# Graph queries and values as high and low products, values masked once a pair through DRAM, and edge steps spread

## The reference, cut to what matters

```python
self_feat = concat(v, q) @ W_self.T + b_self            # q is 0 where a row of v sums to 0
for d in range(2):                                      # d = 1 uses the transposed adjacency
    A = adj if d == 0 else swapaxes(adj, 1, 2)
    A = A[:, :, :20, :]
    cond, vb = A.sum(-1), A @ w_bias + b_bias           # 11 labels a cell: the "edges"
    kv = self_feat[:, :20]
    qh = (self_feat @ Wq[d].T + bq[d]).reshape(B, N, 16, 8)
    kh = (kv @ Wk[d].T + bk[d]).reshape(B, 20, 16, 8)
    aff = einsum('bnhd,bmhd->bnhm', qh, kh) / sqrt(8)
    aff = where(cond > 0, aff, NEG) + vb
    w = softmax(aff, axis=-1)
    out_t = einsum('bnhm,bmf->bnhf', w, kv)
    output += einsum('bnhf,hgf->bnhg', out_t, Wout[d]) + bout[d]
result = v + relu(output)
```

## Time and profile before

| | |
|---|---|
| median of 3 runs | 608.84 us (607.85 to 609.20) |
| the profiled execution, its own time | 608.95 us |
| its span | 607.4 us |
| granted TensorE clock, mean | 0.998 |
| instructions in the span | 17246 |
| HBM read, written | 25.74 MB, 6.31 MB |

### The profile page before, as it was taken

The page is one execution under the profiler, slowest core; times in us unless marked ns, Lnnn a source line. Parts: engine busy times, 40 slices in busy tenths (PEclk is TensorE's granted clock), DMA queues, the critical chain, the costliest instruction groups (busy, mean ns, idle before and its releaser), DMA issues.

```text
span 607.4 us, 17246 instructions
## 1 busy us (share of the span) xinstructions
PE 594.2 (98%) x5570; PEld 538.0 (89%) x5570; DVE 514.0 (85%) x1132; ACT 466.5 (77%) x1703; POOL 291.1 (48%) x355
## 2 busy tenths in 40 slices
PE   8999999999999999999999999999998999999996
PEld 8889999999999999999999999888887888888886
DVE  5899989888988988998998998888867878888876
ACT  4888887988889789789889879778776566566563
POOL 4445435435435435345354354556643554554551
PEclk9999999999999999999999999999999999999999
DMA  8210210210210210210201202133421212212101
GB/s 239 82 40 9 49 50 10 57 46 9 56 41 15 56 37 19 56 31 24 56 13 42 64 2 57 53 96 105 131 86 54 69 38 71 60 44 69 54 17 36
DMA packets 54678, 32.55 MB, mean 54 GB/s; under 512 B 15200, under 2 KB 52464, under 8 KB 54640
## 3 DMA queue, kind: packets, MB, share of 16 engines
q1 hardware_dynamic: 53008, 27.85, 16.9%
q0 software_dynamic: 1632, 4.21, 2.2%
HBM read 25.74 MB, written 6.31 MB: 53 GB/s over the span
## 4 chain that ended last, share of the span: by engine, by line
PE 88%; DVE 6%; ACT 3%; issue 1%; DMA 1%; POOL 0%; ACTq 0%; DVEq 0%; SPq 0%; POOLq 0%
PE banks L701 10%; PE banks L731 10%; PE banks L714 9%; PE banks L2084 7%; PE banks L669 5%; PE banks L673 5%; PE banks L670 5%; PE banks L2056 4%; PE banks L2070 3%; PE banks L685 2%; PE banks L754 2%; PE banks L1501 2%; PE banks L755 2%; PE banks L756 2%; PE banks L2044 2%; PE banks L2031 2%
## 5 line engine op out<-in xcount | busy, mean ns | idle before, releaser
L593 POOL TENSOR_TENSOR late_blocks<-late_blocks,p_rsum 128x512 f32<-128x512 f32 x96 | 99.0, 1052 | 156.9 <-DVE p_rsum L1076 156.9
L928 ACT ACTIVATE late_blocks<-banks,neg_max 128x128 f32<-128x128 f32 x384 | 137.1, 402 | 27.9 <-DVE neg_max L1070 27.9
L928 ACT ACTIVATION_READ_ACCUMULATOR late_blocks<-banks,neg_max 128x1 f32 x384 | 93.2, 243 | 0.0
L909 ACT ACTIVATE wide<-banks 128x512 f32<-128x512 f32 x124 | 75.6, 610 | 5.5 <-PE banks L673 4.4
L669 PE MATMUL banks<-xT_hi,w_qkv_hi 128*128 128x256 f32 x256 | 77.7, 304 | 0.0
L1070 DVE TENSOR_REDUCE neg_max<-banks 128x8 f32<-128x1024 f32 x64 | 76.5, 1195 | 1.3 <-PE banks L701 1.3
L673 PE MATMUL banks<-xT_hi,w_qkv_lo 128*128 128x256 f32 x256 | 72.2, 282 | 0.0
L670 PE MATMUL banks<-xT_lo,w_qkv_hi 128*128 128x256 f32 x256 | 71.9, 281 | 0.0
L701 PE MATMUL banks<-wide 64*128 64x128 f32 x1024 | 66.0, 278 | 0.2
L701 PEld LDWEIGHTS banks<-wide 64*128 64x128 f32 x1024 | 59.8, 188 | 6.1 <-issue 3.5
L928 ACT ACTIVATE third_p<-banks,neg_max 128x128 f32<-128x128 f32 x128 | 47.0, 387 | 20.0 <-DVE neg_max L1070 20.0
(11 more groups left out here) (172 smaller groups left out, 1700.7 us busy)
## 6 DMA issues: line engine op xcount, KB each, us to landing
early<-in_mask SPq DMA_DIRECT2D x16, 220.0 KB
early<-in_mask SPq DMA_DIRECT2D x80, 44.0 KB
x_in<-in_x SPq DMA_DIRECT2D x16, 128.0 KB, 2.2
x_res<-in_x SPq DMA_DIRECT2D x16, 128.0 KB, 2.2
x_scratch<-x SPq DMA_DIRECT2D x16, 128.0 KB, 1.9
f_x_in<-x_scratch SPq DMA_DIRECT2D x16, 128.0 KB, 2.5
f_x_res<-x_scratch POOLq DMA_DIRECT2D x16, 128.0 KB, 2.8
x_scratch<-f_x POOLq DMA_DIRECT2D x16, 128.0 KB, 2.2
```

The costliest lines, as they stand in the source:

```text
L593: pool.tensor_tensor(p[:, heads, :], p[:, heads, :], p_rsum[:, b, heads].unsqueeze(2).broadcast_to([128, 4, T]), ALU.mult).then_inc(p_read ...
L909: act.activation(qk_dst(name) if name[0] == "q" else v_dst(name), work_ps[bank], ACT.Copy).then_inc(bank_free[bank], 1)
L928: act.activation(p[:, m, :], s_ps[b][:, e, j, :], ACT.Exp, bias=neg_max[:, b, 4 * e + j:4 * e + j + 1], accum_out=p_sum[:, b, m:m + 1]).th ...
```

## The change

- **Queries.** ScalarE writes the turned self features as the high part (`selfT_hi`, fp32r); VectorE computes the low part from the same PSUM tile (`split_selfT`). Query weights and `Wout` are split once by POOL, in attention body 1 (`split_weights`). Queries are three products for each d.
- **Order of tokens.** The two sequences of a pair are interleaved in the turned self features (`by_token`), so the 40 neighbour tokens are the first 40 columns. The transposes of `turn_self` write every second element of PSUM, and the saves of queries and keys read every second.
- **Values.** One product for a pair (three fp32r products of 288 columns, 40 rows). ScalarE saves it to `v_rows`; SP stores it block by block onto the diagonal of a cleared DRAM image, waits, and loads the whole image part back into `v_block`. `copy_keys`, the mask and the maskings go. The image is cleared in attention body 14.
- **TensorE's order** in a body: `turn_w(s,0)`, `self_features`, `affinity(s+1,0)`, `weights_v(s,0)`, `turn_self`, `turn_w(s,1)`, `affinity(s+1,1)`, `keys`, `turn_x`, `values(s+2)`, `queries(s+2)`, `weights_v(s,1)`.
- **Places of the new steps.** On ScalarE `save_v(s+2)` stands after `save_xT(s+3)` and before the exponential of (s+1,0). On VectorE `split_selfT(s+2)` stands after the scaling of (s,0) and before the bias of (s+1,0).
- **Last body.** Seven more fill products; half of the last save of turned weights goes from ScalarE to VectorE.
- **Edges.** The last label sum is halved over feed-forward bodies 2 and 3, and the three steps of `make_bias` go to bodies 10, 11 and 12.

```diff
+    def sum_last_labels(dve, part):
+        blocks = CELLS // TS // 2
+        at = slice(part * blocks, part * blocks + blocks)
+        dve.wait_ge(cells_weighted, PAIRS)
+        last = dve.reduce_sum(sums_of(PAIRS - 1, 1)[:, at],
+                              val.rearrange("p (j k) l -> p j k l", k=TS)[:, at], AX.X)
...
-            if at(s, 3):
-                edges.parts["sum_labels"](dve, PAIRS - 1)
-            if at(s, PAIRS - 6):
-                edges.parts["make_bias"](dve)
+            for part in range(2):
+                if at(s, 2 + part):
+                    edges.parts["sum_last_labels"](dve, part)
+            for part in range(3):
+                if at(s, PAIRS - 6 + part):
+                    edges.parts["make_bias"](dve, part)
...
         begin.queries(pair(0))
+        begin.values(pair(0))
         output(pair(PAIRS - 2))
...
+        begin.wait_values(2)
         output(pair(PAIRS - 1))
...
         begin.queries(pair(1))
+        begin.values(pair(1))
...
         begin.save_self(pair(0))
         residual(pair(PAIRS - 3))
+        begin.split_selfT(pair(0))
...
         begin.row_max(pair(0), 0)
+        begin.split_selfT(pair(1))
         begin.shift_scores(pair(0), 0)
         residual(pair(PAIRS - 2))
...
     def set_constants(dve):
-        dve.wait_ge(mask_steps, 1 + 2 * GCH)
-        for n in range(2):
-            for b in range(2):
-                dve.tensor_copy(v_block[:, n, b, :, :, GD],
-                                v_mask[:, :, 0].unsqueeze(1).broadcast_to([KC, 2, GH]))
+        dve.memset(v_rows[:], 1.0)
+        dve.memset(v_block[:], 0.0).then_inc(v_cleared, 1)
...
+    def split_weights(pool, which):
+        hi, lo, raw = ((wq_hi, wq_lo, g.gqk_w[:, 0:2, :]),
+                       (wo_hi, wo_lo, g.gout_w[:].rearrange("p d v -> p (d v)")))[which]
+        pool.tensor_copy(hi[:], raw).then_inc(weights_high, 1)
+        pool.wait_ge(weights_high, which + 1)
+        pool.tensor_tensor(lo[:], raw, hi[:].bitcast(F32), ALU.subtract).then_inc(weights_split, 1)
...
+        def move_values(s):
+            if at(s, 0):
+                sp.wait_ge(v_image_cleared, 2 * 16)
+            zero_wait(sp, v_loaded[s.par], s.half * 16)
+            sp.wait_ge(v_saved, s.n * 2 + 2)
+            for b in range(2):
+                sp.dma_start(v_diagonal(s.par, b),
+                             v_rows[b:BM:2].rearrange("p s d c v -> p s (d c v)")
+                             ).then_inc(v_stored[s.par], 16)
+            sp.wait_ge(v_stored[s.par], s.half * 32 + 32)
+            zero_wait(sp, out_full, unit_count(step_from(s, -2), 1))
+            sp.dma_start(v_block[:, s.par].rearrange("p b s d c v -> p b (s d c v)"),
+                         v_whole(s.par)).then_inc(v_loaded[s.par], 16)
...
-                last = pe.transpose(turns_ps[:, b * T:b * T + T], self_nat[:, s.par, b, :], g.ident[:])
+                last = pe.transpose(by_token(turns_ps[:, 0:2 * T])[:, b], self_nat[:, s.par, b, :], g.ident[:])
...
+            pe.wait_ge(selfT_split, s.n + 1)
             for d in range(2):
-                last = pe.matmul(turns_ps[:, d * 2 * T:d * 2 * T + 2 * T], g.gqk_w[:, d, :],
-                                 selfT[:].rearrange("p b t -> p (b t)"), start=True, stop=True)
+                dst = turns_ps[:, d * 2 * T:d * 2 * T + 2 * T]
+                pe.matmul(dst, wq_hi[:, d, :], selfT_hi[:], start=True, stop=False)
+                pe.matmul(dst, wq_lo[:, d, :], selfT_hi[:], start=False, stop=False)
+                last = pe.matmul(dst, wq_hi[:, d, :], selfT_lo[:], start=False, stop=True)
...
+        def values(s):
+            zero_wait(pe, o_ready, unit_count(step_from(s, -2), 0))
+            pe.wait_ge(selfT_split, s.n + 1)
+            dst, near = v_ps.rearrange("p d s c v -> p (d s c v)"), slice(0, 2 * NG)
+            pe.matmul(dst, selfT_hi[:, near], wo_hi[:], start=True, stop=False)
+            pe.matmul(dst, selfT_hi[:, near], wo_lo[:], start=False, stop=False)
+            pe.matmul(dst, selfT_lo[:, near], wo_hi[:], start=False, stop=True).then_inc(v_full, 1)
...
         def weights_v(s, b):
-            pe.wait_ge(v_saved, unit_count(s, b))
+            if b == 0:
+                pe.wait_ge(v_loaded[s.par], s.half * 16 + 16)
+            zero_wait(pe, o_ready, unit_count(s, b) - 1)
+            if b == 1 and more(s, 2):
+                pe.wait_ge(v_saved, s.n * 2 + 6)
...
         def save_selfT(s):
+            act.activation(selfT_hi[:], turns_ps[:, 0:2 * T], ACT.Identity, bias=g.b_selfT[:])
+            act.activation(kvT[:], turns_ps[:, 0:2 * NG], ACT.Identity, bias=g.b_selfT[:]).then_inc(kv_saved, 1)
...
+        def save_v(s):
+            act.wait_ge(v_full, s.n + 1)
+            for d in range(2):
+                act.activation(v_rows[:, :, d, :, 0:GD], v_ps[:, d], ACT.Copy).then_inc(v_saved, 1)
...
+        def split_selfT(s):
+            dve.wait_ge(kv_saved, s.n + 1)
+            dve.scalar_tensor_tensor(out=selfT_lo[:], in0=turns_ps[:, 0:2 * T], scalar=g.b_selfT[:],
+                                     in1=selfT_hi[:].bitcast(F32), op0=ALU.add,
+                                     op1=ALU.subtract).then_inc(selfT_split, 1)
```

More of the change, by code:

```diff
@@ L327, in sum_labels @@
         dve.reduce_sum(sums_of(i, 1), val.rearrange("p (j k) l -> p j k l", k=TS), AX.X).then_inc(labels_summed, 1)
+    def sum_last_labels(dve, part):
[4 more added lines that the diff above has]
+                              val.rearrange("p (j k) l -> p j k l", k=TS)[:, at], AX.X)
+        if part == 1:
+            last.then_inc(labels_summed, 1)
     def wait_raw_free(sp, i):
@@ L339, in turn_sums, with make_bias @@
         last.then_inc(sums_turned, 1)
-    def make_bias(dve):
+    def make_bias(dve, part):
         first = slice(0, PAIRS * BM)
[L344 to L347, removed]
+        if part == 0:
+            dve.wait_ge(labels_summed, PAIRS)
+            dve.tensor_scalar(off, g.sums[:, 0, first], 0.0, NEG, ALU.is_le, ALU.mult).then_inc(off_made, 1)
+            return
+        if part == 1:
+            dve.wait_ge(off_made, 1)
+            dve.scalar_tensor_tensor(out=off, in0=g.sums[:, 1, first], scalar=g.b_bias[:], in1=off,
+                                     op0=ALU.add, op1=ALU.add).then_inc(off_made, 1)
+            return
         dve.wait_ge(off_made, 2)
@@ L546, in body @@
                 fed.load(F1)
+                graph.parts["clear_images"](sp)
             if more(s, -1):
@@ L602, in body @@
                 edges.parts["weigh"](pool, s.n - 1)
+            if at(s, 1):
+                graph.parts["split_weights"](pool, 0)
             if more(s, 2):
@@ L611, in body @@
             normalise(s, 1, 1)
+            if at(s, 1):
+                graph.parts["split_weights"](pool, 1)
             normalise(step_from(s, 1), 0, 0)
@@ L618, in gpsimd @@
         rstd_of(FIRST)
-        graph.parts["mask_values"](pool)
         setup.parts["split_unscaled"](pool, 4)
@@ L1615, in scalar @@
         begin.save_q(pair(0))
-        begin.copy_keys(pair(0))
+        begin.save_v(pair(0))
         gate(pair(PAIRS - 2))
@@ L1625, in scalar @@
         begin.save_q(pair(1))
-        begin.copy_keys(pair(1))
+        begin.save_v(pair(1))
     def vector(dve, steps=False):
@@ L1920, in body @@
                     load_res(step_from(s, 1))
+            if more(s, 2):
+                move_values(step_from(s, 2))
         for n in range(2):
@@ L2098, in body @@
             if at(s, PAIRS - 1):
-                values(s, 0)
-                values(s, 1)
+                multiply_identity(turns_ps[:, 0:T], FILL + 2)
             if here:
@@ L2103, in body @@
             if at(s, PAIRS - 1):
-                multiply_identity()
+                multiply_identity(g.bank[0][:, 512:512 + T], FILL)
             if second:
                 self_features(step_from(s, 2))
-            if here and not at(s, PAIRS - 1):
-                values(s, 0)
             if nxt:
@@ L2118, in body @@
             if at(s, PAIRS - 1):
-                multiply_identity()
-            if more(s, 3):
-                turn_x(step_from(s, 3))
-            if here and not at(s, PAIRS - 1):
-                values(s, 1)
+                multiply_identity(g.bank[0][:, 512:512 + T], FILL)
             if nxt:
@@ L2127, in body @@
                 keys(step_from(s, 2))
+            if more(s, 3):
+                turn_x(step_from(s, 3))
+            if second:
+                values(step_from(s, 2))
                 queries(step_from(s, 2))
@@ L2134, in tensor @@
             begin.turn_x, begin.self_features, begin.turn_self = turn_x, self_features, turn_self
-            begin.keys, begin.queries, begin.affinity = keys, queries, affinity
+            begin.keys, begin.queries, begin.values, begin.affinity = keys, queries, values, affinity
             begin.wait_keys = lambda count: pe.wait_ge(k_saved, count)
+            begin.wait_values = lambda count: pe.wait_ge(v_saved, count)
             return begin
```

(9 more changed lines are left out.)

134 lines of the change are left out of this document (65 added, 69 removed).

## The result

The changed kernel takes 606.62 us (median; 605.04 to 608.71), the kernel before 608.2 (607.34 to 609.2) beside it, a ratio of 0.9978 [0.9967, 0.9988]. The forecast was 597.8, its range 593.0 to 603.5. The profiled execution took 605.52, its span is 603.9.

A forecast was written before the change was run, and what follows sets the result against it. TensorE, busy 98% of the span, was taken as the bound. Terms +0.3 - 1.3 - 0.5 + 1.4 - 0.8 - 8.5 - 1.7 = -11.1 from 608.95 gave 597.9, forecast as 597.8 us, range 593.0 to 603.5.

The forecast's parts named there:

- the loop's first part: Graph body, TensorE: from the first transposes through features, affinity and weights-times-values to the self transposes, ending at 3.38 us.
- the term 13 x (8.45 - 9.1) = -8.5: Graph bodies 1 to 13: each body falls from 9.1 to 8.45 us, -8.5 us in all.
- Weights-times-values 1.46 for 1.26: Graph body, TensorE: the first such product, held 0.2 us until masking was done, was to lose that stall.
- TensorE's own path: Graph body: TensorE by itself would end its second weights-times-values at 8.24 us, ready at about 8.3.
- The rival of restarts: Graph body: new TensorE waits each cost a restart such as 0.2 us; body 8.8, total 602.3; chance 22%.
- my own case: Graph body of 8.45 us, set by a loop through TensorE, VectorE and ScalarE; total 597.8; chance 50%.
- the five waits that the rival named: Graph body, TensorE: split for x, values and queries, x's copy for queries, values loaded; each costing a restart.
- Attention stage: Memsets replace four small copies on VectorE, which is 1.4 us late once; its idle time absorbs most: +0.3 us.
- Feed-forward stage: Spreading the edge steps gives -1.3 us, halving the last label sum -0.5 us.
- Handover and body 0: Handover to the graph: pair 1's split delays residual and body 0's features, +1.4 us; body 0 itself -0.8.
- the end's gain: From body 14's first transposes to the last operation: four maskings leave VectorE, 17.5 to 15.8 us, -1.7.
- the double cost of interleaved PSUM: Graph body: writing and reading every second PSUM element at half rate makes a body 9.3, total 611.0; chance 5%.

The follow-up runs named there:

- experiment 1: The changed kernel with keys first: ScalarE saves the keys before the next pair's exponential instead of behind it; 600.94 us, ratio 0.9874.
- experiment 11: The kernel of experiment 1 with TensorE's transpose of x moved ahead of the keys product; 600.92 us, ratio 0.9891.
- experiment 4: The changed kernel with the attention stage's two memsets of the value tiles done by POOL instead of VectorE; 606.12 us, ratio 0.9957.
- experiment 3: The kernel before with only the two edge edits (bias in three parts, last label sum in two); 606.8 us, ratio 0.9975.
- Experiment 5: The changed kernel with pair 1's low part moved, on VectorE in the handover, behind pair 14's residual, sum and test; 605.29 us, ratio 0.9948.
- experiment 10: The kernel of Experiment 5 with TensorE's transpose of pair 2's x moved behind pair 1's keys, values ahead of queries; 604.26 us, ratio 0.9934.
- 7: The changed kernel with the edits of experiment 1, experiment 4 and Experiment 5 together; 601.49 us, ratio 0.9875.
- 8: The kernel of experiment 7 with VectorE's bias for the next sequence also moved ahead of the low part; 600.39 us, ratio 0.9871.
- Experiment 9: The changed kernel with twelve unread identity products on TensorE in the handover, before its wait for pair 1's low part; 605.19 us, ratio 0.9954.

## Why the prediction was wrong

**The step that failed is the loop's first part, "weights-times-values to 3.13, the transposes of self 0.25 to 3.38"**, and with it the term 13 x (8.45 - 9.1) = -8.5, which measured -2.8: 5.7 of the 7.6 us between forecast and profiled execution. The self transposes end 527.85 - 523.89 = 3.96 into the body. From ScalarE's start on them the loop is as I had it: 4.83 forecast to the next transposes, 532.77 - 527.89 = 4.88 measured, through the wait of VectorE for the high part, low part, bias, maximum, shift, exponential and keys. The 0.58 ahead of it is three terms, of which ScalarE's earlier start gives 0.16 back:

- *First transposes 0.87 for 0.68.* I gave the stall behind saved keys "about 0.05"; a restart costs 0.19. Keys first takes it away.
- *Features 0.64 for 0.45.* I had the saved queries in time "by 0.05". They were done at 523.73 + 0.84 = 524.57, and the features' weight load started at 524.68, when it should have been over. Keys first takes it away too, with the queries saved at 523.45. It is no echo of the first restart: in experiment 11 there are bodies with the transposes at 0.84 and the features at 0.45 to 0.47, and others with 0.68 and 0.63. That a product is late when its input comes in time by less than a weight load is my reading of these rows.
- *Weights-times-values 1.46 for 1.26.* I had put the 0.2 down to the masking of values, and taken it off. There is no masking now and the 0.2 is still there. The trace of before names the masking as what ended it, that of after names nothing, for the same row (waits of the weight loads, 500 to 560 us; before, then after):

```profile
PEld banks L2084 <- DVE g_v_block L2248: 1.0, 6, 0.2
```

```profile
PEld banks L2151 <- issue: 1.0, 6, 0.2
```

It comes behind the affinity products of 64 rows, as do 0.2 at the keys' load. For the keys experiment 11 shows that it goes with the place: they took 0.57 there and take 0.37 to 0.39, once 0.46, behind x's transposes, which in their turn go from 0.26 to 0.37 (the profile puts some of that down to the low part). For weights-times-values the place is all that I have; no run took its 0.2 away.

These 0.2 also set TensorE's own path, which I had at 8.24: without either restart it is 8.52 (experiment 1), 0.2 of that here and 0.1 between x's transposes and the end of the queries.

**The rival of restarts had the right price, at the wrong places.** "Waits pile up" had a body of 8.8 by restarts of 0.2, and 8.88 it is; my own case charged one restart at 0.05 and one at nothing. But the two that lengthen the body stand behind saved keys and saved queries, neither among the five waits that the rival named. Of its five, only the queries' wait for x's copy costs a restart (0.38 for 0.12), and x's copy comes earlier by about as much. That the body agrees is part luck. With 8.88 in its sum, and the other terms as forecast, the rival gives 602.3 + 13 x 0.08 = 603.3, just inside my range and still 2.2 under the profiled execution.

**Attention stage: +1.0 for +0.3.** The memsets took 0.33 + 1.14 = 1.47 us, less than my 1.8, but I let VectorE's idle time and the work in hand absorb them. The copy of v behind them was needed at once, and TensorE waited 1.1 for it (experiment 4). The Trainium skill, VectorE: DVE Perf Modes, section "Zero memsets can be issued as uint32 (trn2)", has one cycle per element. At that page's 0.96 GHz this is 1.04 ns, an estimate; here 324 elements in 0.33 us agree (1.02 ns each), and 1296 in 1.14 us are a little faster (0.88).

**Feed-forward stage: -1.5 for -1.8**, borne out by experiment 3 (-1.4 for both edits together); the wait that is left is 0.3. How the missing 0.3 divides between the two edits no run shows.

**Handover and body 0: +1.4 for +0.6.** The residual of pair 14 started at 458.45, where I had 458.7; but this trace runs 0.5 ahead of that of before as the handover begins, so on the scale of the forecast it is 458.9. Body 0's features start at 461.20 before and 462.57 after, which with the same 0.5 makes +1.9 for the handover (forecast +1.4) and leaves -0.5 for body 0 (forecast -0.8). What I didn't follow was the second reader: I followed the new split through VectorE's queue, down to the residual, and overlooked that TensorE's transpose of x waits for the split and stands ahead of other work in its own queue. Experiment 5 repeats that oversight, experiment 10 mends it.

**The clock: not foreseen at all.** The wait of 1.9 us, with 0.7 beside it, lets TensorE idle for 2.6 of 4 us (1.2 before, where the wait was for the saved self features), and in three of four executions the mean clock is below 0.998. In the five profiled executions that show it (experiments 1, 4, 7, 8 and 11), the granted clock halves behind this stretch for some 3.4 us, in experiment 4 for over 6. Experiment 9 sets this at 1.4 us of the median.

**Right:** the loop through VectorE and ScalarE behind the self transposes; query products 0.12 (but for the first) and values 0.13 each; the end's gain (-1.6 for -1.7); the loaded values are never a releaser (303.8 KB land in 3.3 us); the transposes that write every second element take the same 0.25, and the queries saved from there the same 0.84, which excludes the double cost of interleaved PSUM.

## What to carry to other kernels

When TensorE is nearly full, taking work off it shows the loop right behind it: follow who saves what its next step reads, in that engine's order, before pricing the gain, and price a wait that is met late, or with less than a weight load in hand, at a restart (0.2 us here) and not at its own length. A stall in the trace is only saved if the releaser named for it is its cause; if another row of the same kind has the stall without that releaser, keep it in the sum. A step moved on one engine has to be followed through all queues that wait for it. Idle time on TensorE is paid for twice if the clock falls behind it: products that nothing reads, put into the wait, bought 1.4 us here. Shortening the wait kept the clock up too (experiment 10).

## What the runs showed of the hardware

- A restart of TensorE behind a short wait: the same six transposes take 0.87 instead of 0.68, the same four feature products 0.64 instead of 0.45, the first query product 0.38 instead of 0.12.
- Four products of the keys take 0.57 right behind the affinity products of 64 rows, and 0.37 to 0.39, once 0.46, with x's transposes between.
- The granted clock falls from 1.00 to 0.50 behind a stretch in which TensorE was busy 1.54 of 4 us, for over 6 us in the profiled execution of experiment 4 (mean 0.993, as in four of its eight). With TensorE busy throughout that stretch no execution of five has a mean under 0.998.
- Two stores in pieces of 216 bytes and one load of 303.8 KB per pair (100 GB/s where the earlier trace rows have 58) cost no other transfer on the queue anything that TensorE waited for; the 128 KB row load still lands in 3.0 us.
